# A new set of urgencies, and an offset for each tile's second layer, for the planner that fixes every engine's order of work

## The reference, cut to what matters

```
x = L0_attn_x; xn = layernorm(x)
x = x + L0_attn(xn) + L0_ffn(xn)
xn = layernorm(x)
x = x + L1_attn(xn) + L1_ffn(xn)
```

## Time and profile before

| | |
|---|---|
| median of 3 runs | 1553.8 us (1552.49 to 1560.11) |
| span of the profiled execution | 1555.3 us |
| TensorE busy, share of the span | 1455.5 us, 94% |
| VectorE busy | 1172.1 us, 75% |
| ScalarE busy | 1036.4 us, 67% |
| GpSimd busy | 325.6 us, 21% |
| mean granted TensorE clock | 0.992 of full |

### The profile page before, as it was taken

One profiled execution on the slowest core, in us unless ns is written; L12 is line 12 of the kernel. 1 busy time (PEld: TensorE's weight loads), 2 busy tenths in 40 slices (PEclk: granted clock), 3 DMA queues, 4 the chain that ended last, 5 costly groups with the idle time before them and its releaser, 6 DMA issues.

```text
span 1555.3 us, 20979 instructions
## 1 busy us (share of the span) xinstructions
PE 1455.5 (94%) x6278; PEld 981.7 (63%) x6278; DVE 1172.1 (75%) x1437; ACT 1036.4 (67%) x2501; POOL 325.6 (21%) x251
## 2 busy tenths in 40 slices
PE   6999999999999999899998999999899999999986
PEld 4767667666556655566555655665567766777764
DVE  3434573596799969998867789979977998957844
ACT  7456637656777677667866786678677677666551
POOL 0001203021101311101411141220125333443320
PEclk9999999999999999999999999999999999999989
DMA  6754435334354434443343443244336544545433
GB/s 243 267 206 172 132 121 180 106 120 145 116 147 150 149 97 131 140 132 102 113 124 122 126 112 122 94 124 140 112 107 179 172 127 133 153 142 156 156 108 111
DMA packets 109676, 217.32 MB, mean 140 GB/s; under 512 B 13688, under 2 KB 57421, under 8 KB 108077
## 3 DMA queue, kind: packets, MB, share of 16 engines
q1 hardware_dynamic: 105020, 206.60, 42.8%
q0 software_dynamic: 4544, 9.38, 1.8%
HBM read 168.81 MB, written 39.93 MB: 134 GB/s over the span
## 4 chain that ended last, share of the span: by engine, by line
PE 36%; issue 27%; DVE 18%; ACT 10%; POOL 7%; DMA 2%; POOLq 0%; SPq 0%; ACTq 0%; DVEq 0%
PE bank L1286 7%; PE bank L1274 5%; PE bank L1276 5%; PE bank L1275 4%; DVE TA L1016 4%; POOL ytok L977 4%; PE bank L1364 3%; DVE AM L1020 3%; POOL RSTD L962 3%; DVE SH L1151 2%; PE bank L1446 2%; PE bank L1426 2%; DVE AM L1024 2%; PE bank L1452 2%; ACT ROWS L798 2%
## 5 line engine op out<-in xcount | busy, mean ns | idle before, releaser
L962 POOL TENSOR_TENSOR RSTD<-SS,power_half 128x4 f32<-128x4 f32 x96 | 135.5, 1411 | 934.2 <-ACT ROWS L798 934.0
L1274 PE MATMUL bank<-NH,GU 128*128 128x512 f32 x512 | 265.5, 518 | 1.9 <-DVE SH L1151 1.8
L1286 PE MATMUL bank<-SH,WD 128*128 128x512 f32 x512 | 261.3, 592 | 0.9 <-DMA WD<-in_w_d 0.9
L1151 DVE TENSOR_TENSOR SH<-SH,bank 128x512 f32<-128x512 f32 x256 | 171.4, 682 | 107.5 <-ACT SH L789 65.8
L798 ACT ACTIVATE ROWS<-bank,root_eps 128x128 f32<-128x128 f32 x384 | 135.8, 368 | 138.0 <-PE bank L1364 137.8
L1016 DVE TENSOR_TENSOR TA<-QK 128x2048 f32<-128x2048 f32 x96 | 219.7, 2288 | 1.2
L789 ACT ACTIVATE SH<-bank 128x512 f32<-128x512 f32 x256 | 151.4, 602 | 88.0 <-PE bank L1276 85.6
L1276 PE MATMUL bank<-NL,GU 128*128 128x512 f32 x512 | 202.2, 395 | 0.0
L1275 PE MATMUL bank<-NH,GU 128*128 128x512 f32 x512 | 201.4, 393 | 0.0
L1020 DVE TENSOR_TENSOR AM<-AM,TA 128x1024 f32<-128x1024 f32 x128 | 152.7, 1219 | 0.8
L1488 PE MATMUL bank<-XT,GU 128*128 128x256 f32 x624 | 146.3, 380 | 1.1 <-DVE SH L1258 0.6
(11 more groups left out here) (211 smaller groups left out, 2526.5 us busy)
## 6 DMA issues: line engine op xcount, KB each, us to landing
GU<-halves SPq DMA_DIRECT2D x112, 512.0 KB, 4.2
GU<-in_w_gu SPq DMA_DIRECT2D x39, 512.0 KB, 3.8
xg<-in_c_fill SPq DMA_DIRECT2D x8, 2080.0 KB
WD<-in_w_d SPq DMA_DIRECT2D x128, 128.0 KB, 2.2
QK<-QK SPq DMA_DIRECT2D x32, 480.0 KB
WD<-in_w_d SPq DMA_DIRECT2D x39, 256.0 KB, 4.0
halves<-GU SPq DMA_DIRECT2D x8, 1024.0 KB, 8.5
FC<-ready_w SPq DMA_DIRECT2D x32, 256.0 KB
```

The costliest lines, as they stand in the source:

```text
L962: pool.tensor_tensor(RSTD[:], SS[:], (power_one if k[0] == "at" else power_half)[:], ALU.pow).then_inc(power_done, 1)
L1151: dve.tensor_tensor(SH[:, g % 4, :], SH[:, g % 4, :], banks[2 + g % 2][:], ALU.mult).then_inc(h_ready, 1)
L1274: pe.matmul(out, w_hi, x_hi, start=True, stop=False)
L1286: pe.matmul(banks[4][:], WD1[:, slot, :], SH[:, g % 4, :], start=first, stop=last).then_inc(down_done, 1)
```

## The change

All urgencies are replaced and gathered in one table. What is new in form: the second layer's urgency has an offset of its own for each of the eight tiles, and rises from layer to layer (+9.03) where it fell before (-2.38); the first-layer numbers spread over hundreds of units where they spread over tens; and the four preparation steps of the second layer's weights are tied in their order (each `load_prep` after the one before it, each `prep` after the one before it). No step is added or removed, no part's planned length changes, and FIRST, READY and the buffers stay.

```diff
+TUNE = {
+    "early": 79.79,
+    "norm0": (19.56, -67.01),
+    "keys": (55.69, -268.19),
+    "kv_sum": -29.26,
+    "query": (74.31, 107.34),
+    "attn": (-107.74, -250.78),
+    "norm1": (-157.5, 120.18),
+    "ffn2": (-1.22, -330.28),
+    "norm2": (119.69, -438.01),
+    "route": (-16.04, -324.82),
+    "norm3": (-288.62, -228.07),
+    "start": (2.15, -17.92),
+    "layer": 9.03,
+    "tile": (-19.89, 17.5, -324.75, -87.96, -61.76, 57.52, -18.67, 302.74),
+    "late": 482.96,
+    "pace": 0.66,
+    "prep": (18.23, -249.56, 16.13, -320.11),
+}
...
-    PREPS = (10.93, 13.41, 18.42, 42.36)
     for l in range(LAYERS):
-        step("load_prep", l, PREPS[l], [(SP, 0.1)], [("raw", 3, SP, 2.0)] + ([("prep", l - 2, ACT_)] if l > 1 else []))
-        step("prep", l, PREPS[l] + 8, [(PE, 2.4, ("6", "7")), (DVE, 0.1), (ACT_, 3.1, (), ("6", "7"))],
-             [("load_prep", l, SP, 12.0)] + ([("keep_prep", l - 2, SP, 3.0)] if l > 1 else []))
-        step("keep_prep", l, PREPS[l] + 9, [(SP, 0.1)], [("prep", l, ACT_)])
+        step("load_prep", l, TUNE["prep"][l], [(SP, 0.1)], [("raw", 3, SP, 2.0)] + ([("load_prep", l - 1, SP)] if l else []) + ([("prep", l - 2, ACT_)] if l > 1 else []))
+        step("prep", l, TUNE["prep"][l] + 8, [(PE, 2.4, ("6", "7")), (DVE, 0.1), (ACT_, 3.1, (), ("6", "7"))],
+             [("load_prep", l, SP, 12.0)] + ([("keep_prep", l - 2, SP, 3.0)] if l > 1 else []) + ([("prep", l - 1, ACT_)] if l else []))
+        step("keep_prep", l, TUNE["prep"][l] + 9, [(SP, 0.1)], [("prep", l, ACT_)])
...
-    EARLY = 60.0
-    NORM0 = (0.22, -59.59)
-    KEYS = (-0.03, 10.16)
-    KV_SUM = 13.39
-    QUERY = (37.58, 14.61)
-    ATTN = (-6.27, 31.95)
-    NORM1 = (23.92, 60.26)
-    FFN2 = (67.27, -31.99)
-    NORM2 = (9.93, 112.22)
-    ROUTE = (-26.39, 14.62)
-    NORM3 = (-37.1, 32.53)
...
-        a = b * HALVES * SPAN - EARLY
+        a = b * HALVES * SPAN - TUNE["early"]
...
-    START = (36.84, 38.37)
-    LATENCY = -2.38
...
-            u, key = b * HALVES * SPAN + START[h] + LATENCY * l, (t, l)
+            u, key = b * HALVES * SPAN + TUNE["start"][h] + TUNE["tile"][t] + TUNE["layer"] * l, (t, l)
...
-    LATE, PACE = 236.33, 0.74
...
-        u = LATE + PACE * g
+        u = TUNE["late"] + TUNE["pace"] * g
```

More of the change, by code:

```diff
@@ L240, in schedule @@
             after += [("raw", 0, SP, 3.0)]
-        scaling(a + NORM0[h], "n0", (t,), after, [(ACT_, 0.5), (DVE, 0.6, (), ("LN",))])
-        step("keys", t, a + KEYS[h], [(PE, 2.8, ("6", "7")), (DVE, 1.2, (), ("6", "7"))],
+        scaling(a + TUNE["norm0"][h], "n0", (t,), after, [(ACT_, 0.5), (DVE, 0.6, (), ("LN",))])
+        step("keys", t, a + TUNE["keys"][h], [(PE, 2.8, ("6", "7")), (DVE, 1.2, (), ("6", "7"))],
              [("normed", ("n0", t), DVE), ("split_attn", 0, DVE)] + last("keys", DVE) + ([("kv_sum", b - 1, PE)] if b else []))
-        step("keys_exp", t, a + KEYS[h] + 0.2, [(ACT_, 2.4, ("exp", "table"), ("table",)), (DVE, 0.6, (), ("exp",))], [("keys", t, DVE)])
+        step("keys_exp", t, a + TUNE["keys"][h] + 0.2, [(ACT_, 2.4, ("exp", "table"), ("table",)), (DVE, 0.6, (), ("exp",))], [("keys", t, DVE)])
         if h:
-            step("kv_sum", b, a + KV_SUM, [(PE, 1.8, ("6",)), (ACT_, 0.16, (), ("6",))],
+            step("kv_sum", b, a + TUNE["kv_sum"], [(PE, 1.8, ("6",)), (ACT_, 0.16, (), ("6",))],
                  [("keys_exp", t, DVE), ("keys_exp", t - 1, DVE)] + ([("centre", ("at", t - 2), PE)] if b else []))
-        step("query", t, a + QUERY[h], [(PE, 0.7, ("7", "QP")), (ACT_, 3.25, ("exp", "table"), ("7", "table")), (DVE, 0.6, (), ("exp",))],
+        step("query", t, a + TUNE["query"][h], [(PE, 0.7, ("7", "QP")), (ACT_, 3.25, ("exp", "table"), ("7", "table")), (DVE, 0.6, (), ("exp",))],
              [("normed", ("n0", t), DVE), ("split_attn", 0, DVE)] + last_scaling("n1", "centre", PE))
-        scaling(a + ATTN[h], "at", (t,), [("query", t, DVE), ("kv_sum", b, ACT_)] + last_scaling("n1", "centre", PE),
+        scaling(a + TUNE["attn"][h], "at", (t,), [("query", t, DVE), ("kv_sum", b, ACT_)] + last_scaling("n1", "centre", PE),
                 [(DVE, 1.25, ("exp",), ("LN",))])
-        scaling(a + NORM1[h], "n1", (t,), [("normed", ("at", t), DVE)] + last("ffn2_add", DVE)
+        scaling(a + TUNE["norm1"][h], "n1", (t,), [("normed", ("at", t), DVE)] + last("ffn2_add", DVE)
                 + ([("split", EXPERTS - 1, DVE)] if not t else []),
@@ L255, in schedule @@
         for c in range(3):
-            step("ffn2", (t, c), a + FFN2[h] + 0.8 * c,
+            step("ffn2", (t, c), a + TUNE["ffn2"][h] + 0.8 * c,
                  [(PE, 1.39, ("6", "7"), (), (), -0.5), (ACT_, 0.59, ("table",), ("table",)), (DVE, 0.67, (), ("6", "7"))],
                  [("normed", ("n1", t), DVE)] + ([("ffn2", (t, c - 1), PE)] if c else last("ffn2_down", PE)))
-        step("ffn2_down", t, a + FFN2[h] + 3.0, [(PE, 2.6, ("6", "YF"))],
+        step("ffn2_down", t, a + TUNE["ffn2"][h] + 3.0, [(PE, 2.6, ("6", "YF"))],
              [("ffn2", (t, c), DVE) for c in range(3)] + last("ffn2_down", PE) + ([("scatter", (t - 1, 7), POOL, 3.0)] if t else []))
-        step("ffn2_add", t, a + FFN2[h] + 3.0, [(DVE, 0.67, (), ("6",))], [("ffn2_down", t, PE)])
-        scaling(a + NORM2[h], "n2", (t,), [("ffn2_add", t, DVE)], [(DVE, 0.67, (), ("LN",))])
-        scaling(a + NORM3[h], "n3", (t,), [("normed", ("n2", t), DVE), ("add_experts", t, DVE)] + last_scaling("n3", "normed", ACT_),
+        step("ffn2_add", t, a + TUNE["ffn2"][h] + 3.0, [(DVE, 0.67, (), ("6",))], [("ffn2_down", t, PE)])
+        scaling(a + TUNE["norm2"][h], "n2", (t,), [("ffn2_add", t, DVE)], [(DVE, 0.67, (), ("LN",))])
+        scaling(a + TUNE["norm3"][h], "n3", (t,), [("normed", ("n2", t), DVE), ("add_experts", t, DVE)] + last_scaling("n3", "normed", ACT_),
                 [(ACT_, 0.5, (), ("LN",))])
-        step("logits", t, a + NORM3[h] + 4.0, [(PE, 0.9, ("6",)), (ACT_, 0.1, (), ("6",))],
+        step("logits", t, a + TUNE["norm3"][h] + 4.0, [(PE, 0.9, ("6",)), (ACT_, 0.1, (), ("6",))],
              [("normed", ("n3", t), ACT_)] + ([("route", (t - 1, 3), DVE)] if t else []))
-        r = a + NORM3[h] + ROUTE[h]
+        r = a + TUNE["norm3"][h] + TUNE["route"][h]
         step("route", (t, 0), r, [(DVE, 0.15), (ACT_, 1.4, ("table",), ("table",))], [("logits", t, ACT_)])
```

## The result

The changed kernel takes 1547.5 us at the median of 6 runs (1543.8 to 1551.1), the kernel before 1554.8 us in 6 runs beside them (1552.5 to 1560.1). The ratio is 0.9935, with a 95% interval of 0.9919 to 0.9951. So it is faster, by 0.65%, where 1.7% was forecast. The two medians by themselves lie 7.3 us apart, 0.47%, so the size of the gain is known only as 0.5 to 0.8%. 1547.5 us is inside the range of 1500 to 1572, but the step is less than half of the one forecast.

A forecast was written before the change was run, and what follows sets the result against it. TensorE, busy 1455.5 of 1555.3 us, was taken as the bound, leaving 99.8 us idle. Gains of 14 (middle), 6 (routed) and 7 (tail) sum to 27 us: 1528.3 profiled, so 1527 us predicted, range 1500 to 1572.

The forecast's parts named there:

- the middle: From 300 us to the last tile's Z at 1130.7: 14 us less TensorE idle time, bounds 28 us and nothing.
- the routed stretch: From 1130.7 to 1505.2 us: 6 us less TensorE idle time by the middle's rule, bounds 12 and 0.
- The tail: Last 50.1 us, with 20.1 us idle: a third filled, 7 us gained, bounds 14 us and nothing.
- The start: Tile 0's second layer: first view up to 12 us sooner after the norm; in itself moves no end.
- The preparation steps: Second-layer weight preparation, first step held until expert step 26: priced at nothing, up to 12 us lost if the last is late.
- Busy time: Whole kernel: TensorE's 1455.5 us busy stay, as no product is added or removed; only 99.8 us idle recoverable.
- The 64 us hidden in the first product: Expert steps: first of three like products shows 518 ns against 393, 64 us of hidden slack, left out of the sum.
- The larger gain: Rival: a quarter of the hidden 64 us gives way too, 1511 us, below 1500 with best bounds; below 1505, chance 0.10.
- That idle time would only be moved about: Rival, whole kernel: the order moves idle time but removes none, 1546 to 1562 us; chance 0.15.
- The last tile's second layer: Rival, end of kernel: this chain falls behind the routed blocks, costing 46 us, time 1580; chance 0.08.
- Table loads: ScalarE: ten loads more or less are 13 us, a third counted, 4 us either way, zero in the sum.
- the power on GpSimd: Collisions with VectorE products: 10 us at the end, zero in the sum; part of the other-stalls rival, 1565 to 1580, chance 0.13.

The follow-up runs named there:

- the lighter VectorE: Both kernels with each layer's four short ham adds on 64 of 512 columns: ratio 0.9878 on the kernel before, 0.9850 on the changed kernel.
- The three runs in which the balance was undone: Changed kernel with blocks starting at urgency 480.0 (1.0098) or second-layer offsets all 0 (1.0105); kernel before with only first-layer and preparation numbers new (1.0358).
- the repeat: The changed kernel itself run once more, unaltered, on another chip as a yardstick: ratio 0.9924 against the kernel before.
- late480: The changed kernel with the routed blocks starting at urgency 480.0 instead of 482.96: ratio 1.0098 against the kernel before.
- late490: The changed kernel with the routed blocks starting at urgency 490 instead of 482.96: ratio 0.9970 against the kernel before.
- old_tile2: The kernel before with tile 2's second layer given the offset -324.75 and the preparation steps tied in a chain: ratio 1.0078.
- first_only: The kernel before with only the first-layer and preparation numbers new, second-layer and block urgencies as before: ratio 1.0358.

## Why the prediction was wrong

The direction was right; the size was not, and the sum failed at one rule, applied to two stretches.

**The step that failed** is the middle: "give 300 to 1130.7 half of the way from its idle share to that of 50 to 300", 14 us. It took the 1.7% of the stretch from 50 to 300 as something that an order can bring about later too. Measured is 1.3 us. The idle share of the middle was 4.6 to 5.6% in every order. It was lower only when VectorE had less to do, at 4.0 and 4.2%; silu for gelu left it at 4.8 and 4.7%. The prediction had a reason in hand, since it says that VectorE stays over 80% busy whatever the order, and took half where nearly nothing was due. How much of that share is VectorE's load, and what holds the rest, is not shown. The 6 us of the routed stretch came by the same rule and went the same way: 1.3 us more idle time instead of 6 less. There the lighter VectorE changed nothing, while silu for gelu took the idle time from 18.7 to 13.2 us and from 20.0 to 16.1, so nothing shows VectorE's load as the cause there. Which part of ScalarE's work counts stays open.

**The tail** was of the right kind and too small: 7 us forecast, 13.1 measured, near the bound of 14, and the clock back at 1.00, where above 0.86 was forecast. That the total is off by 21 us and not by 27 is owed to this error the other way. The three runs in which the balance was undone brought the idle end back, 18 to 50 us of it.

**The start.** The first view comes at 169.0 instead of 177.1, 23 us after tile 0's Z instead of 41, and the first layer ends 34 us sooner. As forecast this moved no end in itself. What it should have saved later did not show: the stretch from 50 to 300, priced at nothing, has 2.2 us more idle time, and the number of layers done by the last Z copy went from 20 to 19. The preparation steps were priced at nothing with up to 12 us lost; alone on the old order they cost 0.64% (8 to 10 us), with 4.0 us of the wait for weights uncovered. In the changed kernel filling that wait again won nothing.

**Busy time.** That TensorE's 1455.5 us would stay was nearly so: 1460.9 in this profile and 1457.3 in that of the repeat. Yet the sum has nothing for the 5.4 us, which is nearly half of the idle time that the change took away. Part of it goes with the clock: 0.989 over 1549.2 us is short of full speed by 17.0 us and 0.992 over 1555.3 us by 12.4 us. The 64 us hidden in the first product of an expert's three stay: 519 ns against 397 ns for the second, times 512, 62 us. The larger gain that was to come out of them did not, and neither the weight loads' share of 63% nor the 94% told how much an order can recover.

**The rivals.** That idle time would only be moved about was right for all but the tail, and its range, 1546 to 1562, holds the measured 1547.5. The last tile's second layer did not fall behind the blocks by much: in the changed kernel's order 30 of them come before that tile's last layer, where by the prediction's own reckoning 32 should. `late480` shows how near the point of decision was: 2.96 units of urgency turn the gain of 0.65% into a loss of 1%. The margin that the prediction read from the old trace, three blocks at the last layer, was no margin in the new order. Table loads went up by eight, worth 1 to 2 us by the estimate above; the power on GpSimd, with a median of 1.15 us instead of 1.05, was not tested by itself.

**Open** is why single steps away from the old order cost 0.6 to 0.8%, while the whole of them gains. The planner's lengths foresaw the two shifts of the blocks well (`late480` 23.5 us behind the changed kernel and 25 measured, `late490` 4.8 and 5.4, from the ratios) and the rest badly: `old_tile2` 3.1 us faster than the old order where it is 11 to 12 us slower, and the change as a whole 32.4 us where the chip gave 7 to 10. No run assigns the difference. The prediction did not ask the planner for its own end; it would have been further off than the sum above.

## What to carry to other kernels

Price a new order by what holds the idle time in each stretch, and not by the best stretch of the same kernel: here an order recovered next to nothing where VectorE was 79 to 86% busy, and less work on VectorE recovered a part. Look first at the end, where a chain runs alone after the bulk is done; that is where this order paid, and where a slight shift lost it again. When a planner's order is tuned to the last per cent, treat the kernel that you start from as one draw among many, and measure several near-equal orders instead of trusting the best-ranked one.

## What was not expected of the hardware

The mean granted clock was 0.83 over 80 to 100 us in the changed kernel with only 3.7 us of idle time in them, 3.66 of them one wait for weights. In the repeat of the same kernel it was 0.91 with 3.6 us of idle time, so nearly the same wait went with another mean clock. Over the last 116 us of `first_only`, in which TensorE is shown busy for 65.6 us, it was 0.76. In both, the busy time counts work at the lower of the two levels, so the busy share understates what such a hole costs.
